# A new order for the first twenty microseconds of an RWKV and gated-FFN layer, and identity products on TensorE ahead of and between the transposes

## What is computed

```python
xn = layernorm(x)                                   # over the 1024 channels
k, r = xn @ Wk.T, xn @ Wr.T                         # 1024 x 1024 each
y = wkv_scan(-exp(time_decay), time_first, k, v=r)  # a recurrence over the 4096 tokens
att = (sigmoid(r) * y) @ Wo.T
h = silu(xn @ wg.T / 127) * (xn @ wu.T / 127)       # 3072 hidden, int32 weights
out = x + att + (h @ wd.T) / 127
```

## Time and profile before

| What | Value |
|---|---|
| Median of the runs | 1359.35 us |
| The profiled execution's own time | 1359.52 us |
| Its span, slowest core (core 3) | 1358.0 us |
| Spans of the 8 cores | 1355.6 to 1358.0 us |
| TensorE busy | 1334.7 us, 98% of the span, 6208 products |
| VectorE busy | 674.6 us, 50% |
| ScalarE busy | 396.5 us, 29% |
| DMA in the first of 40 slices | 0.9 of the 16 engines |

### The profile page before, as it was taken

How to read it: one execution, slowest core, us unless ns; L and a number is a source line. 1 busy time by engine, 2 the same in 40 slices (tenths; PEclk the granted TensorE clock), 3 DMA queues, 4 the chain that set the end, 5 groups by cost and what they waited for, 6 DMA issues and landing times.

```text
span 1358.0 us, 17854 instructions; the slowest of 8 cores (1355.6 to 1358.0 us)
## 1 busy us (share of the span) xinstructions
PE 1334.7 (98%) x6208; PEld 606.6 (45%) x6208; DVE 674.6 (50%) x1101; ACT 396.5 (29%) x663; POOL 35.2 (3%) x70
## 2 busy tenths in 40 slices
PE   4999999999999999999999999999999999999999
PEld 2444444444444444444444444444444444444444
DVE  4666666515952288323873238721487215672211
ACT  5554545312331233212332123221233212221100
POOL 0111111000000000000000000000000000000000
PEclk9999999999999999999999999999999999999999
DMA  9699989953554544545545444544455443334411
GB/s 231 144 183 196 209 163 181 204 142 120 167 144 148 168 137 135 147 150 176 125 117 163 155 156 124 143 152 156 150 143 126 155 155 124 94 102 164 153 47 55
DMA packets 90376, 200.41 MB, mean 148 GB/s; under 512 B 32816, under 2 KB 35888, under 8 KB 90160
## 3 DMA queue, kind: packets, MB, share of 16 engines
q1 hardware_dynamic: 55584, 167.81, 39.0%
q0 software_dynamic: 9360, 25.17, 12.5%
q10 hardware_dynamic: 25344, 6.29, 2.5%
HBM read 184.56 MB, written 33.55 MB: 161 GB/s over the span
## 4 chain that ended last, share of the span: by engine, by line
PE 98%; DMA 2%; SPq 0%; issue 0%; DVE 0%; DVEq 0%; POOLq 0%
PE ps L309 33%; PE ps L313 33%; PE ps_o L327 24%; PE ps_o L334 8%; DMA ring<-w_gu 1%; DMA x_buf<-x_tm 1%; PE ps L291 0%; SPq L170 0%; DVE xres L556 0%; DVEq L555 0%; POOLq L255 0%
## 5 line engine op out<-in xcount | busy, mean ns | idle before, releaser
L309 PE MATMUL ps<-xn,ring 128*128 128x512 bf16 x2048 | 485.5, 380 | 4.1 <-DMA ring<-w_gu 3.9
L313 PE MATMUL ps<-xn,ring 128*128 128x512 bf16 x2048 | 484.7, 379 | 0.0
L549 DVE SCALAR_TENSOR_TENSOR h_act<-ps,silu 128x512 bf16<-128x512 f32 x192 | 132.5, 690 | 438.4 <-PE ps L313 427.5
L327 PE MATMUL ps_o<-wd_bf,h_act 128*128 128x512 bf16 x1536 | 342.0, 379 | 0.0
L309 PEld LDWEIGHTS ps<-xn,ring 128*128 128x128 bf16 x2048 | 200.5, 98 | 246.1 <-issue 6.2
L313 PEld LDWEIGHTS ps<-xn,ring 128*128 128x128 bf16 x2048 | 200.7, 98 | 242.6 <-issue 1.7
L420 ACT ACTIVATE silu<-ps 128x512 f32<-128x512 f32 x192 | 114.6, 597 | 452.7 <-PE ps L309 452.4
L327 PEld LDWEIGHTS ps_o<-wd_bf,h_act 128*128 128x128 bf16 x1536 | 150.3, 98 | 181.3
L334 PE MATMUL ps_o<-wo_bf,outp 128*128 128x512 bf16 x512 | 120.9, 379 | 0.0
L402 ACT ACTIVATE den<-den 128x512 f32<-128x512 f32 x64 | 40.3, 630 | 260.1 <-DVE den L537 259.9
L556 DVE TENSOR_TENSOR xres<-xres,ps_o 128x512 f32<-128x512 f32 x64 | 44.0, 688 | 87.0 <-PE ps_o L334 86.4
(11 more groups left out here) (40 smaller groups left out, 319.1 us busy)
## 6 DMA issues: line engine op xcount, KB each, us to landing
ring<-gu_bfd SPq DMA_DIRECT2D x144, 512.0 KB, 3.3
ring<-kr_bfd SPq DMA_DIRECT2D x48, 512.0 KB, 3.9
xres<-x_tm SPq DMA_DIRECT2D x64, 256.0 KB, 5.5
out_tm<-xres SPq DMA_DIRECT2D x64, 256.0 KB, 4.7
x_buf<-x_tm SPq DMA_DIRECT2D x28, 512.0 KB, 6.4
ring<-w_gu POOLq DMA_DIRECT2D x24, 512.0 KB, 11.3
gu_bfd<-ring SPq DMA_DIRECT2D x24, 512.0 KB, 7.4
ring<-w_kr POOLq DMA_DIRECT2D x8, 512.0 KB, 7.4
```

The costliest lines, as they stand in the source:

```text
L309: ins = te.matmul(bank(kind, idx, 0), w[:, gc * D:(gc + 1) * D], xn[c % 2][:, gc, :], start=(gc == 0), stop=(gc == G - 1))
L313: ins = te.matmul(bank(kind, idx, 1), w[:, C + gc * D:C + (gc + 1) * D], xn[c % 2][:, gc, :], start=(gc == 0), stop=(gc == G - 1))
L327: te.matmul(ps_o[i % 2], h_act[c % 2][:, hg * TC + tt * D:hg * TC + (tt + 1) * D], wd_bf[:, half, hg * 512:(hg + 1) * 512], start=(hg == 0 ...
L549: ve.scalar_tensor_tensor(out=h_act[c % 2][:, hg * TC:(hg + 1) * TC], in0=bank("gu", i, 1), scalar=1.0 / (127.0 * 127.0), in1=silu[i % 3], ...
```

## The change

SyncE issues x tiles 0 to 3, waits for tile 3 to land, issues tiles 4 and 5, waits for the second weight tile to land, and issues tiles 6 and 7. The two small vectors go out on ScalarE's queue at its start. The residual tiles go out after the ninth weight tile. GpSimd waits for tile 1 in place of tile 3. ScalarE makes `etd`, the exponential of `time_decay`, first of all. On VectorE `ln_nb(l)` now comes ahead of `ln_bn(l + 1)`. The transposes use their own banks (`tr_bank`). The units gu 3, 4 and 5, which need only chunk 1, are cut by tokens: the first 256 columns when tiles 4 and 5 are there (`gu_part`), the others when tiles 6 and 7 are there. Units kr 0 and kr 1 follow one another after them. TensorE multiplies the identity by itself 100 times once the identity exists, and 16 times after each of the first four transposes (`keep_running`).

```diff
-SLOTS = [("tr", l0) for l0 in range(NT)]
-SLOTS += [("gu", 0), ("tr", 4), ("gu", 1), ("tr", 5), ("gu", 2), ("tr", 6), ("tr", 7), ("kr", 0)]
-for s0 in range(1, 2 * G):
+SLOTS = [("gu", i0) for i0 in range(6)] + [("kr", 0), ("kr", 1)]
+for s0 in range(2, 2 * G):
     SLOTS += [("gu", 3 * s0), ("gu", 3 * s0 + 1), ("gu", 3 * s0 + 2), ("kr", s0)]
...
+        def tr_bank(l, k):
+            return pair[2][k] if l in (1, 3) else ps_o[k]
...
-                for l in range(2 * NX):
+                for l in range(NX):
                     x_load(l)
-                sy.dma_start(out=tdt, in_=td_hbm).then_inc(sem["io_td"], 16)
-                sy.dma_start(out=tft, in_=tf_hbm).then_inc(sem["io_tf"], 16)
-                for i in range(3):
-                    res_load(i)
+                sy.wait_ge(*x_landed(3))
+                x_load(NX)
+                x_load(NX + 1)
+                sy.wait_ge(*loaded(1))
+                x_load(NX + 2)
+                x_load(NX + 3)
...
+                            if n == 8:
+                                for i in range(3):
+                                    res_load(i)
...
-                gp.wait_ge(sem["xl3"], 16)
                 for n in range(NS):
+                    if n == 0:
+                        gp.wait_ge(*x_landed(1))
...
+                def evacuated(l, k):
+                    te.wait_ge(sem["v_ev" if k else "s_ev"], l + 1)
...
+                        if l >= 2 and cb % 4 == 0:
+                            evacuated(l - 2 if l < 5 else l - 1, cb // 4)
...
+                def gu_part(i, t0, t1):
+                    c = GU[i][0]
+                    if t0 == 0:
+                        acquire("gu", i)
+                        te.wait_ge(*loaded(RING_AT[("gu", i)]))
+                    w = ring[RING_AT[("gu", i)] % R]
+                    for m in range(2):
+                        for gc in range(G):
+                            if m == 0 and gc % 4 == 0:
+                                evacuated(NT * c + t1 - 1, gc // 4)
+                            ins = te.matmul(bank("gu", i, m)[:, t0 * D:t1 * D],
+                                            w[:, m * C + gc * D:m * C + (gc + 1) * D],
+                                            xn[c][:, gc, t0 * D:t1 * D],
+                                            start=(gc == 0), stop=(gc == G - 1))
+                        if t1 == NT:
+                            ins.then_inc(sem["t_u" if m else "t_g"], 1)
...
+                def keep_running(n):
+                    for _ in range(n):
+                        te.matmul(pair[0][0][:, 0:D], ident, ident, start=True, stop=True)
+
                 te.wait_ge(sem["g_id"], 1)
+                keep_running(100)
                 for l in range(NT):
                     tr(l)
+                    keep_running(16)
                 xn_ready(0)
                 proj("gu", 0, 0, "t_g", "t_u")
                 tr(4)
                 proj("gu", 1, 0, "t_g", "t_u")
                 tr(5)
                 proj("gu", 2, 0, "t_g", "t_u")
+                gu_part(3, 0, 2)
                 tr(6)
+                gu_part(4, 0, 2)
                 tr(7)
-                proj("kr", 0, 0, "t_k", "t_r")
-                xn_ready(1)
-                for s in range(1, 2 * G):
+                gu_part(5, 0, 2)
+                for i in range(3, 6):
+                    gu_part(i, 2, NT)
+                for s in range(2):
+                    proj("kr", s, s, "t_k", "t_r")
+                for s in range(2, 2 * G):
```

More of the change, by code:

```diff
@@ L51 @@
 for kind0, i0 in SLOTS:
-    if kind0 == "tr":
-        continue
     c0, row0 = GU[i0] if kind0 == "gu" else KR[i0]
@@ L278, in acquire @@
                     pk, pi = SLOTS[q - 3]
[L279 to L285, removed]
+                    te.wait_ge(sem["v_h" if pk == "gu" else "v_zA"], pi + 1)
+                def evacuated(l, k):
+                    te.wait_ge(sem["v_ev" if k else "s_ev"], l + 1)
                 def tr(l):
-                    acquire("tr", l)
                     te.wait_ge(sem["s_xt"], l + 1)
                     for cb in range(G):
-                        ins = te.matmul(bank("tr", l, cb // 4)[:, (cb % 4) * D:(cb % 4 + 1) * D],
+                        if l >= 2 and cb % 4 == 0:
+                            evacuated(l - 2 if l < 5 else l - 1, cb // 4)
+                        ins = te.matmul(tr_bank(l, cb // 4)[:, (cb % 4) * D:(cb % 4 + 1) * D],
                                         xt[l % 2][:, cb * D:(cb + 1) * D], ident, start=True, stop=True)
@@ L296, in xn_ready @@
                     if c < 2:
-                        te.wait_ge(sem["s_ev"], NT * (c + 1))
-                        te.wait_ge(sem["v_ev"], NT * (c + 1))
+                        evacuated(NT * c + NT - 1, 0)
+                        evacuated(NT * c + NT - 1, 1)
                     else:
@@ L396, in ln_ev @@
                     sc.wait_ge(sem["t_tr"], l + 1)
-                    sc.copy(out=xn[c % 2][:, 0:4, t * D:(t + 1) * D],
-                            in_=bank("tr", l, 0).rearrange("p (k t) -> p k t", t=D)).then_inc(sem["s_ev"], 1)
+                    sc.copy(out=xn[c][:, 0:4, t * D:(t + 1) * D],
+                            in_=tr_bank(l, 0).rearrange("p (k t) -> p k t", t=D)).then_inc(sem["s_ev"], 1)
                 def att_rec(a):
@@ L421, in gate @@
                                   scale=1.0 / 127.0).then_inc(sem["s_sil"], 1)
+                sc.dma_start(out=tdt, in_=td_hbm).then_inc(sem["io_td"], 16)
+                sc.dma_start(out=tft, in_=tf_hbm).then_inc(sem["io_tf"], 16)
                 sc.wait_ge(sem["v_c"], 1)
+                sc.wait_ge(sem["io_td"], 16)
+                sc.activation(out=etd, in_=tdt, func=Act.Exp).then_inc(sem["s_etd"], 1)
                 ln_rstd(0)
+                ln_xt(0)
                 ln_rstd(1)
-                ln_xt(0)
+                ln_xt(1)
                 ln_rstd(2)
-                ln_xt(1)
                 ln_ev(0)
-                ln_rstd(3)
                 ln_xt(2)
                 ln_ev(1)
-                ln_rstd(4)
+                ln_rstd(3)
                 ln_xt(3)
                 ln_ev(2)
+                ln_ev(3)
+                ln_rstd(4)
+                ln_xt(4)
                 ln_rstd(5)
-                ln_xt(4)
-                ln_ev(3)
-                ln_rstd(6)
                 ln_xt(5)
-                ln_rstd(7)
-                sc.wait_ge(sem["io_td"], 16)
-                sc.activation(out=etd, in_=tdt, func=Act.Exp).then_inc(sem["s_etd"], 1)
                 sc.wait_ge(sem["v_w"], 1)
@@ L447, in _ @@
                 sc.activation(out=euv, in_=tft, func=Act.Exp).then_inc(sem["s_ew"], 1)
+                ln_ev(4)
                 gate(0)
-                ln_ev(4)
+                ln_ev(5)
+                gate(1)
+                gate(2)
+                ln_rstd(6)
                 ln_xt(6)
-                gate(1)
-                ln_ev(5)
+                ln_rstd(7)
                 ln_xt(7)
-                gate(2)
                 ln_ev(6)
                 ln_ev(7)
+                gate(3)
+                gate(4)
+                gate(5)
                 att_exp(0)
-                for s in range(1, 2 * G):
+                att_rec(0)
+                att_exp(1)
+                for s in range(2, 2 * G):
                     for i in range(3 * s, 3 * s + 3):
@@ L502, in ln_ev @@
                     ve.wait_ge(sem["t_tr"], l + 1)
-                    ve.tensor_copy(xn[c % 2][:, 4:8, t * D:(t + 1) * D],
-                                   bank("tr", l, 1).rearrange("p (k t) -> p k t", t=D)).then_inc(sem["v_ev"], 1)
+                    ve.tensor_copy(xn[c][:, 4:8, t * D:(t + 1) * D],
+                                   tr_bank(l, 1).rearrange("p (k t) -> p k t", t=D)).then_inc(sem["v_ev"], 1)
                 def att_max(a):
@@ L562, in _ @@
                 ln_bn(0)
+                ve.wait_ge(sem["s_etd"], 1)
+                ve.tensor_scalar_mul(wv, etd, -1.0).then_inc(sem["v_w"], 1)
+                ln_nb(0)
                 ln_bn(1)
-                ln_nb(0)
+                ln_nb(1)
                 ln_bn(2)
-                ln_nb(1)
+                ln_nb(2)
                 ln_ev(0)
                 ln_bn(3)
-                ln_nb(2)
                 ln_ev(1)
-                ln_bn(4)
                 ln_nb(3)
                 ln_ev(2)
+                ln_ev(3)
+                ln_bn(4)
+                ln_nb(4)
                 ln_bn(5)
-                ln_nb(4)
-                ln_ev(3)
+                ln_nb(5)
+                ln_ev(4)
+                ffn_h(0)
+                ln_ev(5)
+                ffn_h(1)
                 ln_bn(6)
-                ln_nb(5)
+                ffn_h(2)
+                ln_nb(6)
                 ln_bn(7)
-                ln_nb(6)
-                ve.wait_ge(sem["s_etd"], 1)
-                ve.tensor_scalar_mul(wv, etd, -1.0).then_inc(sem["v_w"], 1)
                 ln_nb(7)
[L584 to L589, removed]
```

(9 more changed lines are left out.)

## The result

The changed kernel is slower: 1366.61 us (median of four runs, 1366.27 to 1367.04) against 1359.35, half a per cent more. The ratio is 1.0053, with a 95% interval of 1.0035 to 1.0070. I had forecast 1357.0, in a range of 1355.0 to 1360.5.

The account below looks back on a forecast made before the run. TensorE's dense stretch from the first weight tile on bounds the kernel. Core 3's terms -4.7 - 2.7 - 0.2 + 0.3 + 2.4 + 0.7 + 0.2 + 0.9 = -3.1; slowest span -2.4, so 1359.4 to 1357.0, range 1355.0 to 1360.5.

Parts of the forecast that it names:

- part 3: Tiles 4 to 7: tile 4's transposes 0.3 after gu 0, waits of 2.4 at tile 6 and 0.7 at tile 7.
- the sum: Core 3's terms from all parts, -3.1; the slowest span, core 6 then the slowest, falls 2.4, giving 1357.0.
- Rival A: Tiles 4 to 7 come late behind SyncE's waits, each microsecond past 21.5 costing one; 1364 to 1367, chance 0.15.
- my two bounds: Rates for tiles 4 and 5 beside GpSimd's queue: 0.14 MB/us, or 0.055 to 0.07 MB/us.
- the 0.28 and 0.29 of the earlier trace: MB moved by the two queues from 30 to 32 us, 76 packets each; basis of the high rate.
- Part 1: First tiles, from tile 0's statistics at 5.9 to gu 0 at 19.25 in place of 23.94; gain 4.7.
- Part 2: Identity products keep TensorE's clock up, so gu 0's products run at 1.73 per 8; gain 2.7.
- rival B: The clock isn't up at gu 0: 2.7 not won and 1.3 paid, part hidden; 1360.2, chance 0.10.
- Tile 7's 0.7: TensorE's wait at tile 7's transposes for ScalarE's copy of tile 6, behind tile 7's normalisation; 0.7.
- Part 4: kr 0 and kr 1 together: gu 8 waits for the second zA, costing 0.9 more.
- K: Start of kr 0, forecast at 45.4; the second zA done at K + 14.7, gu 8 due at K + 13.8.

Follow-up runs that it names:

- experiment 3: The change with GpSimd waiting for tile 3, as before, in place of tile 1, SyncE's two waits kept; one run, 1365.54 us.
- experiment 4: The change with the small vectors behind tile 5 on SyncE's queue, their exponential later and a constant Exp at ScalarE's start; 1.0059, 1366.95 us.
- experiments 1 and 2: The change with all x tiles issued at the start: 1.0016, 1361.54 us; the change with only SyncE's first wait removed: 1.0013, 1361.35 us.
- experiment 6: The change with all x tiles at the start, small vectors behind tile 7 on SyncE's queue, their exponentials behind tile 7's last copy; 1.0002, 1359.76 us.
- Experiment 7: experiment 6 plus kr 1 writing the output banks and tile 6's statistics and normalisation ahead of gate 0; 0.9980, 1356.82 us.
- experiment 5: The change with all x tiles at the start, a constant Exp first, and small vectors on ScalarE's queue behind tile 3's normalisation; 1.0042, 1365.34 us.

## Why the prediction was wrong

**The step that failed** is in part 3. It lets tile 4's statistics start behind tile 3's copy and says that "tile 5 follows in time", so the sum has no term for the tiles' landing. Rival A had them at 17.7 and 21.4, "in time by a hair", by 0.14 MB/us, and had 15%. They landed at 24.6 and 29.6. Rival A's rule, that each microsecond past 21.5 costs one, gives 8.1 for tile 5, and tile 6's transposes came 8.5 later than forecast (43.55 against 35.0). Its price, 1364 to 1367, is what was measured. Two sizes were wrong. The time from the issue to the first packet was 4.8 us, where 17.7 leaves room for about 1.7. With nothing of GpSimd's in front it was about 2.3 (experiment 3). The rate was 0.21 MB in 2 us with equal packets, 0.11 MB/us, between my two bounds. I held the 0.28 and 0.29 of the earlier trace rows to be the rate of 4 KB packets. In the change no 2 us from 18 to 30 moved more than 0.23 on SyncE's queue.

**Part 1.** From tile 0's statistics to gu 0 I had 13.35, and it took 13.8, both in the change on core 1 (7.80 to 21.59) and in experiment 4 (5.43 to 19.21). That the latter is so near 19.25 is partly luck, as its tile 0 was there 0.5 earlier than I had assumed. The landing was off by more: 7.70 on the slowest core in place of 5.8. I had allowed 0.1 for the vector. Its queue moved as many packets as the tiles', and 0.43 MB of the tiles passed from 4 to 6 us, against 0.55 in the kernel before.

**Part 2.** gu 0 was fast, as forecast. But the clock was down again behind the waits of 3.67 and 3.29. gu 1 took 1.7 more (29.32 to 34.45 against 3.45), which by the chain cost nothing, as TensorE would have waited the longer for tile 6. The work behind tile 6 took about 1.6 more, and that is on the chain. So rival B, the low clock, came true in another place.

**Part 3.** The table load ahead of tile 6's Ln and the wait came (3.3, forecast 2.4). The load of 1.28 at 39.78 was followed by its Ln at 41.08, so the two loads cost what the sum had for them. Tile 7's 0.7 did not come on core 1: slow products covered it. On core 5, where the products behind tile 6 were fast, it came as 0.5.

**Part 4.** Forecast 0.9, measured 1.1. The part's own terms add up to K + 14.85 and not 14.7, which makes 1.05. Experiment 7 removed this wait together with tile 6's. How the 2.9 us between 6 and 7 divide between the two was not tried.

**The sum on core 1.** TensorE's timeline against the 52.3 of the forecast for the unit after kr 1 is +2.3 at gu 0, +3.4 at tile 4, +1.7 for gu 1's clock, +0.9 at tile 6, +1.6 for its clock, -0.7 at tile 7 = 61.5, measured 61.67. These terms say where TensorE lost the time and not what would bring it back. The first four, 8.3 together, fill the time until tile 6's transposes, which tile 5's landing sets. Taking away the first of them (experiment 4) or adding slow products to gu 0 (the change without identity products) left the time where it was. Undoing SyncE's first wait gives 5 us (experiments 1 and 2). The vectors give about 1.9 more, once nothing waits for them (experiment 6 against 1, with intervals that overlap a little). Experiment 7 shows that the waits at tile 6 and for zA, as experiment 6 had them, were hand-made order and not bytes.

Still open is what the clock itself costs in the end. In no pair did the identity products move the time beyond the intervals.

## What to carry to other kernels

A transfer that is issued behind a wait can lose far more than the wait: here tile 4 moved nothing for 4.8 us, behind what GpSimd's queue had issued meanwhile, and then shared the engines with it. So keep the first tiles' issues ahead of every wait, and put tiny transfers behind them, with what needs them as late in each engine's order as it can go. Where a start is brought forward, look for what each engine stands behind at the new time: a wait of 6.1 in experiment 5 and one of 2.5 with the identity products alone both led to a 4 KB vector. And follow the chain before naming a wait as the cause. The longest wait of TensorE here, 3.67 for tile 4, was not on it.

## What the runs showed that I had not expected

- Two vectors of 4 KB, 128 packets of 32 bytes each, moved as many packets from 4 to 6 us as the x tiles with packets of 4 KB (117 and 117). Issued in midstream one of them took 15.8 us (experiment 5).
- The order of two queues' issues, 0.5 us apart, moved a tile's time to landing from 12.4 to 4.8 and a weight tile's from 7.9 to 10.4 (experiment 3).
- After waits of 2.2, 2.5, 3.3 and 3.7 us TensorE's next products ran near the 1.2 GHz level. But the length of the wait doesn't decide by itself. On core 5 of the change the products behind tile 6's wait of 3.34 were fast. With the identity products alone gu 0 was fast after waits of 2.07 to 2.76 on five cores and slow after 1.96, 2.06 and 2.23 on the three others, in the same execution.
